# Delta attention: the first block products of an inverse on both halves of the partitions, and a new order on all five queues

## The chip, the cores and the metric

One core of one Trainium2 chip runs the whole program. The metric is the device time in microseconds (us) of one execution; the kernel before took 3255.22 us, the median of 3 executions (3253.78 to 3260.65).

## What is computed

The program is a small network on x of shape (4, 1024, 128), all in fp32. Its first and longest layer is a gated delta rule with 8 heads and 3 rank-one updates per token; a mixture of 15 experts, a decay attention and a second mixture follow and are not touched. Cut to what matters, per head and batch:

```python
for t in range(1024):
    S = S * exp(g[t])
    for i in range(3):                       # nh = 3 updates
        kS = k[t, i] @ S
        S = S + beta[t, i] * outer(k[t, i], v[t, i] - kS)
    o[t] = q[t] @ S
```

Before it come projections of x, a causal convolution of 4 taps on each of q, k and v, SiLU and a norm; behind it a norm, a gate and an output projection.

## The kernel before

The function `delta_attention` works in chunks of TC = 32 tokens. With 3 updates a token a chunk has R = 96 rows. A step N takes one head and NCC = 2 chunks of all B = 4 batches, so U = 8 units; there are NS = 128 steps (8 heads by 16). For each unit a 96 x 96 triangular matrix has to be inverted, after which the chunk is a few matrix products with the state S.

The inverse is made in blocks of BLK = 32. The three diagonal blocks are inverted on POOL (`subst`, lines 723 and 726) by forward substitution, for GROUP = 4 steps at a time: 31 pairs of a product and a subtraction, spread over four loop turns by `sub_steps` in 12 spots a turn. They go to DRAM and back (`n_d`, `x_d`, `y_d`), and on the way ACT transposes them once per group (`xt`, line 863). TensorE then joins the blocks: `zm` (line 1204) makes 64 x 64 products for each unit into the PSUM tile ZW, ACT moves them negated into Zt (`zev`, lines 844 and 845), `wm` (line 1213) multiplies Zt with Yf, ACT moves a part (`w12`, line 851), `m3` (line 1221) makes the last block, and `yev` (line 857) moves it to Yf. ZW has 128 x (8 x 64) fp32, one bank of PSUM, of which only partitions 0 to 63 are used.

The loop is a software pipeline. Turn f works on three steps at once: f (projections and taps of k and q), f - 1 (norms, Gram matrix, `kr`, `ap`, stores), c = f - BACK = f - 11 (v, gate, inverse blocks) and r = c - 1 (the recurrence on the state: `ks`, `rhs_`, `w_`, `wev`, `sr`, `sup`, `o_`), plus the output of r - 1. There are NF = 142 turns. In turns 0 to 10 only the k side is live, in turns 12 to 127 everything, from 128 on only the v side and the recurrence.

Each engine runs its queue strictly in the order in which the loop body lists the helpers, and waits at a helper's semaphores (`need`, `wait_ge`); the order is written out by hand for SP (all DMAs), POOL, ACT, DVE and PE. Things that the order has to respect:

- PP has two banks. Tiles v0, v2, k0, k2 use the first, v1, gate, k1, q (k_tile 3) the second; each projection overwrites what the tile before it in that bank left, so `k_tile(f, 1)` waits for ACT's `gate_(c)` (semaphore gate_ev) and `k_tile(f, 3)` for the third tap of k1.
- Each of the 7 convolved tiles needs tap 0 on ACT (line 788) and taps 1 to 3 on DVE (line 953), each tap waiting for the one before.
- TG holds transposes of k (`ktr`), of v (`vtr`) and the Gram matrices (`gram`), in two halves of four units.
- `xt` waits until the group's substitution is finished; the store of `y_d` on SP waits for `xt`.

The loads of the inverse blocks that the change touches (SP):

```python
sp.dma_start(apkB[N % 2][:, :, :], apk_d[slot(N)])...            # L601
for b in range(2):
    o = slice(BLK * b, BLK * (b + 1))
    sp.dma_start(Dd[N % 2][o, :, o], x_d[q, lanes(N, b)]...)...   # L605
```

## Time and profile before

| | |
|---|---|
| median of 3 executions | 3255.22 us |
| the profiled execution | 3252.41 us, its span 3250.6 us |
| busy over the span | PE 94%, DVE 78%, ACT 70%, POOL 60% |
| TensorE clock granted, mean | 0.963 |
| DMA engines busy, mean | about 56% |

The profile is of one execution. A "busy" PE is the union of its matmuls, whose ends are modelled; the start times are the reliable part, and the text mostly uses distances from start to start. PEld is the weight load that belongs to a matmul. An fp32 matmul is two instructions, so the eight products of `zm` are 16 rows. By the slices of the page the delta layer lies between about 100 and 2480 us, and from about 240 to 2350 us all slices look alike.

### The profile page before, as it was taken

The numbers are of one execution on the slowest core, as the hardware profiler recorded it, in microseconds if no ns is written. First come the engines' busy times: TensorE is split into PE (matmuls) and PEld (weight loads), VectorE is DVE, ScalarE is ACT, GpSimd is POOL, SyncE is SP. The second block draws the span as 40 slices with busy tenths as digits, with TensorE's granted clock in tenths as the row PEclk, the third lists the DMA queues.
The fourth block names the chain that finished last, engine by engine and source line by source line (L and its number), as shares of the span: only waits on it lengthen the run. The fifth ranks groups of instructions, "written<-read, shape, count | busy, mean of one in ns | idle before, by whom it ended". The sixth has DMA issues, their size and how long they took to land. (4 is left out here: it accounts for less than half of the span.)

```text
span 3250.6 us, 83664 instructions
## 1 busy us (share of the span) xinstructions
PE 3046.8 (94%) x27404; PEld 2373.9 (73%) x27404; DVE 2528.6 (78%) x5801; ACT 2265.4 (70%) x6879; POOL 1956.2 (60%) x3107
## 2 busy tenths in 40 slices
PE   5669999999999999999999999999998999768998
PEld 3458888888888888888888888888775444455444
DVE  5669999999999999999999999999654444684443
ACT  4678888888888888888888888888543333323333
POOL 1588888888888888888888888888720000100000
PEclk8779999999999999999999999999998999869999
DMA  4356776767677676767767677766532232002323
GB/s 100 113 153 172 186 183 174 181 173 182 168 190 179 176 181 169 182 174 188 182 170 183 171 175 178 190 180 165 141 95 83 107 145 98 10 2 76 147 98 124
DMA packets 587912, 482.88 MB, mean 149 GB/s; under 512 B 464492, under 2 KB 504076, under 8 KB 581340
## 3 DMA queue, kind: packets, MB, share of 16 engines
q1 hardware_dynamic: 587484, 477.53, 55.5%
q8 instruction: 225, 3.69, 0.5%
q14 instruction: 203, 1.66, 0.2%
HBM read 285.52 MB, written 191.86 MB: 147 GB/s over the span
## 5 line engine op out<-in xcount | busy, mean ns | idle before, releaser
L953 DVE SCALAR_TENSOR_TENSOR conv_k<-PP,tk,conv_k 128x256 f32<-128x256 f32 x1536 | 723.4, 479 | 62.9 <-ACT conv_k L788 35.1
L726 POOL TENSOR_TENSOR X<-X,tmp 96x31 f32<-96x31 f32 (+15 forms) x992 | 534.1, 538 | 77.7
L953 DVE SCALAR_TENSOR_TENSOR conv_v<-PP,tv,conv_v 128x256 f32<-128x256 f32 x1152 | 539.4, 477 | 45.1 <-ACT conv_v L788 35.5
L723 POOL TENSOR_TENSOR tmp<-At,X 96x31 f32<-96x31 f32 (+15 forms) x992 | 486.1, 490 | 63.0 <-DMA At<-n_d 4.8
L1122 PE MATMUL PP<-xn,wk 128*128 128x268 f32 x1024 | 344.6, 421 | 33.7 <-DVE conv_k L953 25.1
L709 POOL TENSOR_TENSOR rk<-ss,half 96x8 f32<-96x8 f32 x128 | 209.5, 1637 | 175.3 <-DVE ss L921 175.3
L691 POOL TENSOR_TENSOR Sg<-S,gend 128x512 f32<-128x512 f32 x256 | 266.1, 1039 | 59.3 <-DVE S L912 59.3
L760 ACT ACTIVATE recA<-TG,es 96x128 f32<-96x128 f32 x1024 | 284.9, 368 | 8.7 <-DVE es L946 8.7
L788 ACT ACTIVATE conv_k<-PP,tk 128x256 f32<-128x256 f32 x512 | 245.1, 480 | 60.1 <-PE PP L1122 53.4
L752 ACT ACTIVATE recA<-TG 128x128 f32<-128x128 f32 x1024 | 265.5, 272 | 25.3 <-PE TG L1173 25.3
L1086 PE MATMUL RB<-rhs,Yf 96*96 96x128 f32 x2048 | 269.1, 274 | 14.6 <-DVE rhs L901 14.3
L778 ACT ACTIVATE ws<-RB 96x512 f32<-96x512 f32 x256 | 151.6, 592 | 183.0 <-PE RB L1086 180.2
L1076 PE MATMUL RA<-S,kqgB 128*96 128x128 f32 x2048 | 276.2, 278 | 1.0 <-DVE S L912 1.0
L1096 PE MATMUL RA<-ws,recB 96*128 96x128 f32 x2048 | 271.1, 275 | 0.2 <-ACT ws L778 0.2
L1086 PEld LDWEIGHTS RB<-rhs,Yf 96*96 96x96 f32 x2048 | 242.2, 163 | 37.0 <-DVE rhs L901 24.6
L1096 PEld LDWEIGHTS RA<-ws,recB 96*128 96x128 f32 x2048 | 259.2, 192 | 8.0 <-ACT ws L778 0.8
L1185 PE MATMUL TG<-kq 128*96 128x128 f32 x1888 | 245.3, 273 | 1.2 <-ACT recA L760 1.0
L1076 PEld LDWEIGHTS RA<-S,kqgB 128*96 128x96 f32 x2048 | 233.4, 163 | 13.0 <-DVE S L912 4.4
L676 POOL TENSOR_TENSOR kqgA<-kq,gdec 128x768 f32<-128x768 f32 x128 | 203.2, 1588 | 39.3 <-ACT kq L829 32.6
L1122 PE MATMUL PP<-xn,wv 128*128 128x268 f32 x768 | 218.5, 391 | 2.3 <-DVE conv_k L953 2.3
L1185 PEld LDWEIGHTS TG<-kq 128*96 128x96 f32 x1888 | 219.0, 163 | 2.2 <-ACT recA L760 2.2
L1122 PEld LDWEIGHTS PP<-xn,wk 128*128 128x128 f32 x1024 | 163.8, 200 | 64.5 <-issue 34.5
(280 smaller groups left out, 6787.9 us busy)
## 6 DMA issues: line engine op xcount, KB each, us to landing
kqg_d<-kqgA SPq DMA_DIRECT2D x128, 512.0 KB, 6.2
kqgB<-kqg_d SPq DMA_DIRECT2D x128, 512.0 KB, 4.3
rec_d<-recA SPq DMA_DIRECT2D x128, 480.0 KB, 3.4
recB<-rec_d SPq DMA_DIRECT2D x128, 480.0 KB, 5.8
f1gates<-f1gates_d SPq DMA_DIRECT2D x24, 1024.0 KB, 6.7
f2gates<-f2gates_d SPq DMA_DIRECT2D x24, 1024.0 KB, 6.7
gdec<-gdec_d SPq DMA_DIRECT2D x128, 128.0 KB, 5.6
apk_d<-apkA SPq DMA_DIRECT2D x128, 128.0 KB, 3.3
```

The lines of the kernel that those rows point to most:

```text
L691: nc.gpsimd.tensor_tensor(Sg[:, :, :], S[cc][:, :, :], d.broadcast_to([128, B, 128]), ALU.mult).then_inc(sg_ev[cc], 1)
L723: nc.gpsimd.tensor_tensor(t, At[q % 2][:, j, j + 1:].unsqueeze(2).broadcast_to(sh), X[q % 2][:, j, 0:cols].unsqueeze(1).broadcast_to(sh), ...
L726: nc.gpsimd.tensor_tensor(x, x, t, ALU.subtract).then_inc(sub_ev, 1)
L752: last = nc.scalar.activation(recA[N % 2][:, u * 128:(u + 1) * 128], TG[:, u, :], ACT.Square, accum_out=ksum[:, u:u + 1])
L760: last = nc.scalar.activation(recA[N % 2][0:R, u * 128:(u + 1) * 128], TG[0:R, u, :], ACT.Copy, scale=es[:, u, TC - 1:TC])
L788: nc.scalar.activation(acc, src[:, :, 0:SPAN], ACT.Copy, scale=w).then_inc(tap0_ev[i], 1)
L953: return nc.vector.scalar_tensor_tensor(acc, src[:, :, j:j + SPAN], w[:, j:j + 1], acc, ALU.mult, ALU.add)
L1076: last = mm(RA[0:R, b, :], kqgB[N % 2][:, b * NCC + cc, 0:R], S[cc][:, b, :], start=True, stop=True)
L1086: last = mm(RB[0:R, b, :], Yf[N % 2][:, b * NCC + cc, :], rhs[:, b, :], start=True, stop=True)
L1096: last = mm(RA[:, b, :], recB[N % 2][:, u * 128:(u + 1) * 128], ws[cc][:, b, :], start=True, stop=True)
L1122: mm(out, w, x, start=True, stop=True).then_inc(tile_mm[i], 1)
L1185: last = mm(gram_bank(N, hf)[0:R, u % HU, :], kq[N % 2][:, u, 0:R], kq[N % 2][:, u, :], start=True, stop=True)
```

## The change

`zm` no longer puts all eight units on partitions 0 to 63. Units 0 to 3 stay there and units 4 to 7 go to partitions 64 to 127 of apkB, Dd and ZW, and the matmuls alternate between the halves, so that they address two row tiles (and with them two column tiles) of the array. The loads of apkB and Dd become 2 + 4 DMAs where there were 1 + 2, of half the size each. ACT's move into Zt becomes four instructions, two for each half. `wm` and `m3` stay as they are and still use partitions 0 to 63 of ZW.

All five loop bodies have a new order. On PE `o_(r, 1)` moves behind the next turn's first v tile, `vtr(c, 0)` too, and `m3` no longer follows `o_(r, 1)` but stands between `k_tile(f, 3)` and `w_(r, 1)`; the Gram products swap. On ACT `xt` moves from the head of the turn to just ahead of `gate_`. On POOL the last substitutions of a group run in the next turn. On DVE `vr(c, 0)` moves into the next turn and `ap` swaps its halves. SP loads first and stores last.

```diff
--- before.py
+++ after.py
@@ -429,7 +429,7 @@
 
         kqgB = two("kqgB", [128, U, 128])
         recB = two("recB", [R, U * 128 + U * TC])
-        apkB, Dd = two("apkB", [64, U, 64]), two("Dd", [64, U, 64])
+        apkB, Dd = two("apkB", [128, HU, 64]), two("Dd", [128, HU, 64])
         Yf = two("Yf", [R, U, R])
         Zt = sb("Zt", [R, U, 64])
         vt = sb("vt", [128, U, R])
@@ -598,11 +598,14 @@
                 need(sp, zm_mm, N - 2)
                 sp.wait_ge(preset_ev, 1)
                 sp.wait_ge(st_ap[N % 2], 4 * uses(N))
-                sp.dma_start(apkB[N % 2][:, :, :], apk_d[slot(N)]).then_inc(ld_da[N % 2], 16)
+                for hf in range(2):
+                    sp.dma_start(apkB[N % 2][64 * hf:64 * hf + 64, :, :], half(apk_d[slot(N)], hf)).then_inc(ld_da[N % 2], 16)
                 sp.wait_ge(st_x[q % 2], uses(q))
                 for b in range(2):
                     o = slice(BLK * b, BLK * (b + 1))
-                    sp.dma_start(Dd[N % 2][o, :, o], x_d[q, lanes(N, b)].rearrange("u r c -> r u c")).then_inc(ld_da[N % 2], 16)
+                    for hf in range(2):
+                        rows = slice(64 * hf + BLK * b, 64 * hf + BLK * b + BLK)
+                        sp.dma_start(Dd[N % 2][rows, :, o], x_d[q, lanes(N, b)][hf * HU:(hf + 1) * HU].rearrange("u r c -> r u c")).then_inc(ld_da[N % 2], 16)
 
             def y_load(N):
                 if not live(N):
@@ -639,16 +642,16 @@
 
             for f in range(NF):
                 r, c = f - BACK - 1, f - BACK
+                rec_load(c)
                 at_load(*group_at(f, GROUP + 1))
                 x_store(*group_at(f, 2 * GROUP + 1))
-                rec_load(c)
+                dec_load(f)
                 da_load(c + 1)
                 weights(*divmod(f, KSTEPS))
-                dec_load(f)
-                kqg_store(f - 1)
+                y_load(c + 1)
                 rec_store(f - 1)
                 ap_store(f - 1)
-                y_load(c + 1)
+                kqg_store(f - 1)
 
         @block.gpsimd
         def _(pool):
@@ -730,14 +733,15 @@
             nc.gpsimd.memset(S[0][:, :, :], 0.0).then_inc(preset_ev, 1)
             for f in range(NF):
                 r, c = f - BACK - 1, f - BACK
+                fo_(r - 1)
+                sg(r, 0)
+                subst(*group_at(f - 1, GROUP + 1), range(10, 12))
+                kqg(f - 1)
+                rk_(f - 1)
+                sg(r, 1)
+                subst(*group_at(f, GROUP + 1), range(0, 9))
                 x_zero(*group_at(f, 3))
-                fo_(r - 1)
-                kqg(f - 1)
-                sg(r, 0)
-                rk_(f - 1)
-                subst(*group_at(f, GROUP + 1), range(0, 6))
-                sg(r, 1)
-                subst(*group_at(f, GROUP + 1), range(6, 12))
+                subst(*group_at(f, GROUP + 1), range(9, 10))
 
         @block.scalar
         def _(act):
@@ -841,8 +845,10 @@
                 need(act, zm_mm, N)
                 need(act, m3_mm, N - 1)
                 act.wait_ge(preset_ev, 1)
-                nc.scalar.activation(Zt[32:64, :, 0:32], ZW[0:32, :, 0:32], ACT.Copy, scale=-1.0)
-                nc.scalar.activation(Zt[64:96, :, :], ZW[32:64, :, :], ACT.Copy, scale=-1.0).then_inc(zev_ev, 1)
+                for hf in range(2):
+                    nc.scalar.activation(half(Zt, hf)[32:64, :, 0:32], ZW[64 * hf:64 * hf + 32, 0:HU, 0:32], ACT.Copy, scale=-1.0)
+                    last = nc.scalar.activation(half(Zt, hf)[64:96, :, :], ZW[64 * hf + 32:64 * hf + 64, 0:HU, :], ACT.Copy, scale=-1.0)
+                last.then_inc(zev_ev, 1)
 
             def w12(N):
                 if not live(N):
@@ -864,27 +870,27 @@
 
             for f in range(NF):
                 r, c = f - BACK - 1, f - BACK
-                xt(*group_at(f, 2 * GROUP + 1))
                 tap0(c, "v0")
+                mo_(r - 1, 1)
+                ksum_(f - 1, 1)
                 tap0(c, "v1")
-                ksum_(f - 1, 1)
                 ksum_(f - 1, 0)
                 wev(r, 0)
                 tap0(c, "v2")
+                xt(*group_at(f, 2 * GROUP + 1))
                 gate_(c)
                 zev(c)
                 tap0(f, "k1")
                 mo_(r, 0)
                 tap0(f, "k0")
+                kr(f - 1, 1)
                 kr(f - 1, 0)
+                w12(c)
+                q2_(f - 1)
+                tap0(f, "k2")
+                tap0(f, "q")
                 vsilu(c)
-                kr(f - 1, 1)
-                tap0(f, "k2")
-                w12(c)
                 wev(r, 1)
-                q2_(f - 1)
-                tap0(f, "q")
-                mo_(r, 1)
                 yev(c)
                 ksilu(f)
                 qsilu(f)
@@ -1020,10 +1026,11 @@
             for f in range(NF):
                 r, c = f - BACK - 1, f - BACK
                 tap1(c, "v0")
+                tap2(c, "v0")
+                vr(c - 1, 0)
+                tap3(c, "v0")
                 osb_(r - 1)
-                tap2(c, "v0")
                 rhs_(r, 0)
-                tap3(c, "v0")
                 tap1(c, "v1")
                 og_(r - 1)
                 tap2(c, "v1")
@@ -1031,30 +1038,29 @@
                 ss_(f - 1)
                 rinv_(f - 1)
                 acc_(r - 1)
+                step_(f - 1)
                 tap1(c, "v2")
-                step_(f - 1)
                 tap2(c, "v2")
                 tap3(c, "v2")
+                es_(f - 1)
                 sup(r, 0)
-                es_(f - 1)
                 tap1(f, "k1")
+                tap2(f, "k1")
                 tap1(f, "k0")
                 tap2(f, "k0")
                 tap3(f, "k0")
+                tap3(f, "k1")
                 rhs_(r, 1)
-                tap2(f, "k1")
-                ap(f - 1, 0)
-                tap3(f, "k1")
+                ap(f - 1, 1)
                 tap1(f, "k2")
                 tap2(f, "k2")
-                ap(f - 1, 1)
                 tap3(f, "k2")
                 tap1(f, "q")
                 tap2(f, "q")
                 tap3(f, "q")
                 vr(c, 1)
+                ap(f - 1, 0)
                 sup(r, 1)
-                vr(c, 0)
 
         @block.tensor
         def _(pe):
@@ -1198,10 +1204,12 @@
             def zm(N):
                 if not live(N):
                     return
-                pe.wait_ge(ld_da[N % 2], 3 * uses(N))
+                pe.wait_ge(ld_da[N % 2], 6 * uses(N))
                 need(pe, yev_ev, N - 1)
-                for u in range(U):
-                    last = mm(ZW[0:64, u, :], apkB[N % 2][:, u, :], Dd[N % 2][:, u, :], start=True, stop=True)
+                for u in range(HU):
+                    for hf in range(2):
+                        o = slice(64 * hf, 64 * hf + 64)
+                        last = mm(ZW[o, u, :], apkB[N % 2][o, u, :], Dd[N % 2][o, u, :], start=True, stop=True)
                 last.then_inc(zm_mm, 1)
 
             def wm(N):
@@ -1238,8 +1246,10 @@
             for f in range(NF):
                 r, c = f - BACK - 1, f - BACK
                 v_tile(c, 0)
+                o_(r - 1, 1)
+                ktr(f - 1, 1)
+                vtr(c - 1, 0)
                 v_tile(c, 1)
-                ktr(f - 1, 1)
                 ks(r, 0)
                 ktr(f - 1, 0)
                 zm(c)
@@ -1254,15 +1264,13 @@
                 k_tile(f, 0)
                 wm(c)
                 ks(r, 1)
+                gram(f - 1, 1)
+                k_tile(f, 2)
+                k_tile(f, 3)
+                m3(c)
+                w_(r, 1)
                 gram(f - 1, 0)
-                k_tile(f, 2)
-                w_(r, 1)
-                gram(f - 1, 1)
-                k_tile(f, 3)
-                o_(r, 1)
-                m3(c)
                 vtr(c, 1)
-                vtr(c, 0)
                 sr(r, 1)
```

## Rows read from the trace of the kernel before

**Rows 1.** Windows view of 1000 to 1500 us: length, each engine's busy time.
```profile
core 0: us, PE busy (x) PEld busy (x) DVE busy (x) ACT busy (x) POOL busy (x), PEclk, DMA share, GB/s
1000.00:1500.00 500.00, 498.20 (x5078) 432.83 (x5081) 460.01 (x1075) 428.13 (x1386) 424.79 (x675) 1.00 0.72 179
```
**Rows 2.** Source view of `zm` (line 1204), 990 to 1500 us.
```profile
L1204 PE MATMUL ZW<-Dd,apkB x464: 218/218/267, 998.8 to 1495.6; 64*64 64x64 f32 x155
```
**Rows 3.** Waits view, 1000 to 1500 us: total us, times, longest.
```profile
PEld PP L1122 <- DVE conv_v L953: 3.4, 7, 0.5
PEld RB L1086 <- DVE rhs L901: 2.9, 7, 0.4
```
**Rows 4.** Timeline of PE in one steady turn: start, length of the group, instructions.
```profile
1016.28 1.14 PE L1204 MATMUL ZW<-Dd,apkB 64*64 64x64 f32 x16
1017.35 0.44 PE L1229 MATMUL SD<-ident,osb 128*128 128x128 f32 x2
...
1020.72 0.62 PE L1122 MATMUL PP<-xn,wk 128*128 128x268 f32 x2
1021.27 0.45 PE L1111 MATMUL SD<-S,kqgB 128*32 128x128 f32 x8
...
1021.87 0.72 PE L1122 MATMUL PP<-xn,wk 128*128 128x268 f32 x2
1022.52 1.15 PE L1213 MATMUL ZW<-Yf,Zt 96*64 96x64 f32 x16
...
1025.42 0.62 PE L1122 MATMUL PP<-xn,wk 128*128 128x268 f32 x2
1025.88 1.04 PE L1086 MATMUL RB<-rhs,Yf 96*96 96x128 f32 x8
...
1028.18 0.45 PE L1111 MATMUL SD<-S,kqgB 128*32 128x128 f32 x8
...
1028.64 0.67 PE L1221 MATMUL ZW<-Yf,Zt 96*32 96x32 f32 x16
1029.24 1.08 PE L1195 MATMUL TG<-ident,vt 128*96 128x128 f32 x8
...
1033.80 0.38 PE L1204 MATMUL ZW<-Dd,apkB 64*64 64x64 f32 x3
```
**Rows 5.** Timeline of PE in the decay attention: 64 x 64 products on four tiles.
```profile
2810.83 1.16 PE L1720 MATMUL b_pair<-b_rF,b_kB 64*64 64x64 f32 x64
2811.92 0.44 PE L1663 MATMUL b_pair<-ident,xT 128*128 128x128 f32 x2
```
**Rows 6.** Timeline of ACT in the same steady turn.
```profile
1019.20 0.46 ACT L788 ACTIVATE conv_v<-PP,tv 128x256 f32<-128x256 f32 x1
1020.02 0.38 ACT L810 ACTIVATE gate<-PP 128x256 f32<-128x256 f32 x1 [0.37 <-PE PP L1122]
1020.43 0.37 ACT L844 ACTIVATE Zt<-ZW 32x256 f32<-32x256 f32 x1
1020.82 0.59 ACT L845 ACTIVATE Zt<-ZW 32x512 f32<-32x512 f32 x1
...
1031.23 2.02 ACT L863 ACTIVATE At<-X 96x1024 f32<-96x1024 f32 x1
```
**Rows 7.** Timeline of SP's queue, same turn: the loads of Dd.
```profile
1018.44 1.08 SPq L605 DMA_DIRECT2D Dd<-x_d  x2
```
**Rows 8.** Timeline of one turn of the start-up.
```profile
156.20 0.42 DVE L946 TENSOR_TENSOR es<-edec,step_s 96x256 f32<-96x256 f32 x1
...
158.51 1.26 PE L1122 MATMUL PP<-xn,wk 128*128 128x268 f32 x2 [3.57 <-DVE conv_k L953]
...
161.27 1.10 PE L1122 MATMUL PP<-xn,wk 128*128 128x268 f32 x2
...
164.47 0.42 ACT L829 ACTIVATE kq<-conv_k 128x256 f32<-128x256 f32 x1 [0.41 <-DVE conv_k L953]
```
**Rows 9.** Timeline of PE in one turn of the run-out.
```profile
2415.16 1.14 PE L1204 MATMUL ZW<-Dd,apkB 64*64 64x64 f32 x16
...
2423.64 1.11 PE L1086 MATMUL RB<-rhs,Yf 96*96 96x128 f32 x8 [0.78 <-DVE rhs L901]
...
2425.43 0.45 PE L1111 MATMUL SD<-S,kqgB 128*32 128x128 f32 x8 [0.68 <-ACT ws L778]
...
2430.29 1.14 PE L1204 MATMUL ZW<-Dd,apkB 64*64 64x64 f32 x16
```

## The prediction

> **What bounds the kernel now.** I read the windows view first, for the long middle of the delta layer. PE is busy 498.20 of 500 us at full clock, DVE 460, ACT 428, POOL 425 [rows 1]. So PE has no gap to speak of, and the others have 1.4 to 2.6 us of slack in a turn. Next the source view of `zm`, which gives the beat: 464 rows are 29 turns of 16, the first starts at 998.8 and the last row of the last turn at 1495.6, about 0.98 behind its first; (1494.6 - 998.8) / 28 = 17.71 us a turn [rows 2]. The timeline of one turn then gives 1033.80 - 1016.28 = 17.52 us [rows 4]. Three turns in four take that, and the fourth, the one in which ACT runs `xt`, takes 4 x 17.71 - 3 x 17.52 = 18.28. The waits view shows that PE's own waits are short: 3.4 and 2.9 us in 28 turns, seven times each, one turn in four [rows 3]. Conclusion: the kernel is set by the length of PE's instruction stream, plus 0.76 us in every fourth turn in which `xt` (2.02 us [rows 6]) holds up ACT's taps. There are 116 full turns (f = 12 to 127, by the code), 10 turns of start-up and 11 of run-out, which have other bounds.
>
> **Part 1, zm on two row tiles.** `zm` starts at 1016.28 and the next group at 1017.35: 1.07 us for 16 instructions [rows 4]. The direct evidence for what tiles do is in the decay attention: 64 instructions of the very same shape, on four tiles, take 2811.92 - 2810.83 = 1.09 us [rows 5]. So four tiles run side by side, each at the pace of the single tile, and neither the weight loads nor the issue are in the way at 17 ns an instruction. Of the 1.07 us some 0.14 is the way out (next part), so a round takes (1.07 - 0.14) / 16 = 0.058 us; two tiles need 8 rounds less, **-0.47 us** a turn. Bounds: 0 (the tiles do not overlap) and -0.47. I take -0.47, as rows 5 are the same shape.
>
> **Part 2, crossings between array shapes.** The timeline shows what a change of the stationary width costs. A k tile followed by `w_` takes 0.46 (1025.42 to 1025.88); followed by the 32-column `o_` it takes 0.55: **0.09 in**. `o_` followed by `m3`, also 32 columns, takes 1028.64 - 1028.18 = 0.46; followed by a k tile 1021.87 - 1021.27 = 0.60: **0.14 out**. That k tile then takes 0.65 up to `wm`, 0.10 more than the 0.46 and 0.09 in explain, which is a tail of the way out [rows 4]. Before, `o_(r, 1)` and `m3` share one stay in the narrow shape. After, `o_(r, 1)` leaves to `ktr` and `m3` enters alone behind a k tile and leaves to `w_`. That is one exit and one entry more: 0.14 + 0.09, and 0 to 0.20 of tails; **+0.34 us** taken, bounds 0.23 and 0.43. The other narrow groups keep their neighbours' shapes. PE's stream becomes 17.52 - 0.47 + 0.34 = 17.39 us.
>
> **Part 3, the other queues, in the three turns without xt.** ACT: from 0.37 us at 256 columns and 0.59 at 512 [rows 6] a half-sized pair takes about 0.27 + 0.37, so four take 1.28 where two took 0.96: +0.32 on an engine with 2.5 us of slack. `wm` waits for it. With w_(r, 0) at 4.8 us into the turn, ws, tap v2 and gate end at about 7.6, the four moves at about 8.95, and `wm` starts at 9.7: covered, by 0.7. DVE: same instructions. `vr(c-1, 0)` fits while DVE waits for `ks` and `ot`, and I find the third tap of each tile ready before the PE tile that wants its bank, the tightest being v1 ahead of the gate tile, at the same distance as before. POOL: same work, its tail moved by some 1.2 us into the next turn. SP: three more DMA issues of about 0.54 us each (1.08 for two [rows 7]), +1.6 us on a queue that otherwise waits; the loads are for the next turn and land with 2 us or more in hand. Cost 0 for all four; if one of these covers is gone, the smallest margin (0 to 0.1 us at the gate tile) is what turns into waits.
>
> **Part 4, xt.** It moves ahead of `gate_`. In the old turn tap v2 starts at 1019.20 and the gate at 1020.02 [rows 6]. With `xt` between them the gate starts at 1019.20 + 0.40 + 1.92 = 1021.52, 1.50 later. PE's k1 tile, which overwrites the gate's bank, starts at 1020.72, 0.24 behind the earliest time that the gate's end (1020.40) allows. So PE stands 1.26 us in every fourth turn, where `xt` cost 0.76 before: **+0.50 in four turns, +0.125 a turn**. Bounds +0.40 and +0.65. Sum of a full turn: -0.47 + 0.34 + 0.125 = **-0.005 us**, over 116 turns -1 us; by the bounds of parts 2 and 4 from -16 to +13.
>
> **Part 5, start-up.** Here a turn is a loop of latencies: es, taps, SiLU, transposes, sums, es. From es (156.20) to the SiLU of q (164.47) are 8.27 us, and the q tile comes 2.76 behind the k2 tile because a Gram product stands between them [rows 8]. After, q follows k2 directly. The k2 tile is itself 0.5 late, as k0's taps come behind two taps of k1. Then DVE's six taps run without a pause, and I count 7.6 to the SiLU of q: -0.65 us for 10 turns, **-6.5** (0 to -13).
>
> **Part 6, run-out.** A turn takes 2430.29 - 2415.16 = 15.13 us, in which PE waits 0.78 for rhs and 0.68 for ws [rows 9]. After, `m3` fills 0.6 of the first wait, the second shrinks by about 0.2, `zm` gives 0.47, the crossings take 0.34, and the longer move into Zt some 0.2: -0.75 for 10 turns, **-7.5** (+2 to -12).
>
> **Sum.** -1 - 6.5 - 7.5 = -15 us on the profiled execution of 3252.4, 3237.4; the median lies 2.8 above that execution. I say 3238.
>
> **The rivals.**
>
> (A) Forecast: the turn is level, the ends gain. 3238, its own range 3216 to 3248. For it: the matching tile rows [rows 5] and a PE without gaps [rows 1].
>
> (B) Level in all: the crossings cost their upper end (+0.09 x 116 = +10) and the start-up gives nothing (+6.5): about 3254, inside 0.2%. For it: every term is of the size of the error of reading starts.
>
> (C) Slower, as the two row tiles do not overlap. The four tiles of rows 5 write their row halves to different banks of PSUM (the h index of the tile), whereas here both halves write one bank, ZW. If TensorE holds one row tile until the other's writes are out, the 0.47 is lost in all 138 live turns: 3238 + 54 for the full turns + about 4 at the run-out, **3296**. It decides if `zm` to `ot` stays above 0.9 us. Against it: in `o_`, four column tiles of one bank run side by side (16 instructions of 128 columns in 0.60 us [rows 4]). The Trainium skill ("TensorEngine Tiling (Array Packing)", section "Restrictions and Gotchas") says that different row tiles cannot access the same PSUM bank at the same time and leaves it to software. By it this layout is unsafe or serial; no row before the change shows two row tiles in one bank, so its chance is small but not nil.
>
> (D) Slower by new waits. DVE is at 92% [rows 1], and a hole of 0.2 us in each turn, at the gate tile or at k0 behind v2's taps, would lengthen every full turn: 3238 + 23 and no gain at the ends, about 3272. It decides from 0.12 us a turn on.
>
> **How the numbers follow.** A 0.62, B 0.19, C 0.06, D 0.13. A measurement tells apart about 0.2%, 6.5 us. Faster (below 3248.7): A without its rim, 0.62. Same: 0.19 and a rim of D, 0.20. Slower: 0.18. The range runs from 3212 (A with the lower ends of parts 2, 4, 5 and 6) to 3265, which takes in B and part of D and leaves out C.
>
> **What would show it.** In the profile after: `zm` to the next group 0.6 us with 16 rows (C: above 0.9); `o_(r, 1)` to `ktr` about 0.60, k3 to `m3` 0.55; three turns at 17.4 and one at 18.65, a mean of 17.7; in the waits view a line of PE waiting for ACT's gate, about 1.2 us once in four turns. If that line is missing, part 4 is wrong and the kernel is some 15 us faster than I say. If the turns without `xt` are above 17.5, look for PE waiting for DVE. Start-up turns should shrink by 0.5 to 1 us, run-out turns from 15.13 to about 14.4.

## The result, and the profile after

The changed kernel takes 3358.03 us (median of 4 executions, 3356.31 to 3361.34) against 3257.93 for the kernel before in the same runs: a ratio of 1.031, 95% interval 1.0292 to 1.0327. It is 100 us slower. I had forecast 3238, with a range up to 3265. The profiled execution took 3356.31 us, its span 3354.5.

The window that was read before, read again:

```profile
core 0: us, PE busy (x) PEld busy (x) DVE busy (x) ACT busy (x) POOL busy (x), PEclk, DMA share, GB/s
1000.00:1500.00 500.00, 476.79 (x4859) 401.45 (x4859) 457.31 (x1027) 412.75 (x1384) 405.66 (x647) 1.00 0.64 171
```

PE was busy 498.20 us there [rows 1] and is busy 476.79 now, at the same granted clock, with 4859 instructions in the window in place of 5078. Every engine has fewer instructions in it: the turns have become longer and PE stands. The source view of `zm` (line 1212 now; durations are those of single instructions in ns):

```profile
L1212 PE MATMUL ZW<-Dd,apkB x432: 218/218/268, 1002.6 to 1485.6; 64*64 64x64 f32 x144
```

These are 27 turns of 16 rows where there were 29 [rows 2]. From the start of one `zm` to the next, over turns 12 to 127, by the place of the turn in its group of four (the third column is the turn in which `xt` costs time; the kernel before runs it at the end of the turn ahead, 14.9 us behind that turn's `zm`):

| | plain | plain | turn of xt | turn behind it | mean |
|---|---|---|---|---|---|
| before | 17.52 | 17.52 | 18.28 | 17.52 | 17.71 |
| predicted | 17.39 | 17.39 | 18.65 | 17.39 | 17.71 |
| after | 17.86 | 17.74 | 18.65 | **20.13** | 18.60 |

0.89 us in 116 turns are 103 us, the whole loss. The waits view of 1000 to 1500 us (total us, times, longest) has lines that are new or much longer, chosen here from the view; before, PE waited 3.4 us for conv_v and 2.9 for rhs [rows 3], and DVE's osb 2.2 us for fo:

```profile
engine line waited for: us in total, times, longest us
POOL tmp L726 <- DMA At<-n_d: 18.8, 7, 3.4
PEld PP L1128 <- DVE conv_v L959: 13.4, 18, 1.1
DVE osb L1006 <- POOL fo L705: 9.8, 7, 2.1
PEld PP L1128 <- ACT gate L814: 8.2, 7, 1.2
PEld SD L1237 <- DVE osb L1006: 5.8, 7, 1.6
```

Seven times in 27 turns is once in a group of four. Three things stand here. The gate line is `xt`, forecast as about 1.2 us once in four turns. The conv_v line is in the turns without `xt`. The lines for At, fo and osb are one chain: POOL waits for the DMA that brings At, so its `fo` comes late, so DVE's osb, so PE's transpose of osb.

The timeline of PE (start, length, instructions, wait before it) shows that the array did what I had worked out:

```profile
1037.32 0.45 PE L1117 MATMUL SD<-S,kqgB 128*32 128x128 f32 x8
...
1037.92 0.66 PE L1179 MATMUL TG<-ident,kq 128*128 128x128 f32 x4
...
1040.71 0.68 PE L1212 MATMUL ZW<-Dd,apkB 64*64 64x64 f32 x16
1041.32 0.44 PE L1237 MATMUL SD<-ident,osb 128*128 128x128 f32 x2
```

`zm` to the next group is 0.61 us with all 16 rows (it was 1.07 [rows 4]; 0.60 was forecast). `o_(r, 1)` to `ktr` is 1037.92 - 1037.32 = 0.60, as forecast. So the loss does not lie in how long `zm` and the crossings take.

### The profile page after: what moved, and what is told of

Read it like the earlier page. It is cut to its first block and busy times, and to the rows that moved or that the text cites. A ratio compares the mean times of both kernels' runs of the same rounds, so it can differ in the third digit from the quotient of the medians.

```text
span 3354.5 us, 84304 instructions
## 1 busy us (share of the span) xinstructions
PE 3044.4 (91%) x27404; PEld 2316.8 (69%) x27404; DVE 2607.7 (78%) x5801; ACT 2279.5 (68%) x7135; POOL 1954.1 (58%) x3107
## 5 line engine op out<-in xcount | busy, mean ns | idle before, releaser
L959 DVE SCALAR_TENSOR_TENSOR conv_k<-PP,tk,conv_k 128x256 f32<-128x256 f32 x1536 | 707.1, 481 | 117.1 <-ACT conv_k L792 84.5
L959 DVE SCALAR_TENSOR_TENSOR conv_v<-PP,tv,conv_v 128x256 f32<-128x256 f32 x1152 | 549.7, 477 | 22.2 <-ACT conv_v L792 3.9
L1128 PE MATMUL PP<-xn,wk 128*128 128x268 f32 x1024 | 324.1, 421 | 118.4 <-DVE conv_k L959 43.6
L1092 PE MATMUL RB<-rhs,Yf 96*96 96x128 f32 x2048 | 282.0, 281 | 7.4 <-DVE rhs L907 5.6
L1128 PEld LDWEIGHTS PP<-xn,wk 128*128 128x128 f32 x1024 | 171.2, 196 | 170.0 <-DVE conv_v L959 56.2
L792 ACT ACTIVATE conv_k<-PP,tk 128x256 f32<-128x256 f32 x512 | 230.0, 474 | 83.1 <-PE PP L1128 76.1
L764 ACT ACTIVATE recA<-TG,es 96x128 f32<-96x128 f32 x1024 | 274.0, 371 | 7.7 <-DVE es L952 7.7
L1082 PEld LDWEIGHTS RA<-S,kqgB 128*96 128x96 f32 x2048 | 240.8, 163 | 22.9 <-DVE S L918 0.9
L1092 PEld LDWEIGHTS RB<-rhs,Yf 96*96 96x96 f32 x2048 | 235.3, 164 | 23.2 <-DVE rhs L907 18.2
L1128 PE MATMUL PP<-xn,wv 128*128 128x268 f32 x768 | 241.5, 395 | 0.0
L756 ACT ACTIVATION_READ_ACCUMULATOR recA<-TG 128x1 f32 x1024 | 213.4, 208 | 0.0
```

Of the source, the lines that this page charges most:

```text
L756: last = nc.scalar.activation(recA[N % 2][:, u * 128:(u + 1) * 128], TG[:, u, :], ACT.Square, accum_out=ksum[:, u:u + 1])
L764: last = nc.scalar.activation(recA[N % 2][0:R, u * 128:(u + 1) * 128], TG[0:R, u, :], ACT.Copy, scale=es[:, u, TC - 1:TC])
L792: nc.scalar.activation(acc, src[:, :, 0:SPAN], ACT.Copy, scale=w).then_inc(tap0_ev[i], 1)
L959: return nc.vector.scalar_tensor_tensor(acc, src[:, :, j:j + SPAN], w[:, j:j + 1], acc, ALU.mult, ALU.add)
L1082: last = mm(RA[0:R, b, :], kqgB[N % 2][:, b * NCC + cc, 0:R], S[cc][:, b, :], start=True, stop=True)
L1092: last = mm(RB[0:R, b, :], Yf[N % 2][:, b * NCC + cc, :], rhs[:, b, :], start=True, stop=True)
```

## The experiments

Each time is a median; the ratio is to the kernel before in the same runs, with its 95% interval. The turns are in the order of the table above: plain, plain, turn of `xt`, turn behind it.

| run | us | ratio | turns | mean |
|---|---|---|---|---|
| e1_tiles_alone | 3239.84 | 0.9958 (0.9939 to 0.9978) | 17.10 17.09 18.28 17.56 | 17.51 |
| e2_orders_alone | 3360.57 | 1.0317 (1.0302 to 1.0332) | 17.87 17.86 19.11 19.74 | 18.64 |
| e3_at_first | 3284.97 | 1.009 (1.007 to 1.011) | 17.86 17.73 18.66 17.69 | 17.98 |
| e4_kqg_later | 3594.75 | 1.1028 (1.0971 to 1.1085) | 20.32 20.47 19.54 20.86 | 20.30 |
| e5_kqg_behind_sg | 3312.92 | 1.0182 (1.0158 to 1.0207) | 17.40 17.40 18.65 19.34 | 18.20 |
| e6_xt_at_head | 3318.2 | 1.019 (1.0167 to 1.0213) | 17.4 17.4 18.68 19.64 | 18.28 |
| e7_tiles_xt_halves | 3221.46 | 0.9896 (0.9864 to 0.9928) | 17.11 17.09 17.09 18.04 | 17.33 |
| e8_xt_halves_alone | 3244.89 | 0.9963 (0.9949 to 0.9977) | 17.52 17.52 17.52 17.77 | 17.58 |
| e9_at_late_before | 3362.75 | 1.0317 (1.0299 to 1.0335) | 17.52 17.52 18.28 21.04 | 18.59 |
| e10_kqg_ahead | 3276.76 | 1.0063 (1.0047 to 1.0079) | 17.41 17.41 19.47 17.40 | 17.92 |
| e11_kqg_ahead_halves | 3244.84 | 0.9961 (0.9947 to 0.9976) | 17.42 17.40 18.47 17.41 | 17.67 |
| e12_tail_behind_sg | **3192.82** | **0.9803** (0.9787 to 0.9819) | 17.10 17.09 17.33 17.13 | 17.16 |

Where `xt` is cut in two, the third number is the turn of its first half and the fourth that of its second.

**The two halves of the change.** e1_tiles_alone is the changed kernel with the loop bodies of the kernel before on all five queues: only the row tiles, their loads and the four moves into Zt are left. e2_orders_alone is the kernel before with the new loop bodies.

> The kernel before with the row-tile form of zm (its split loads and four moves into Zt) and nothing else; all five loop bodies are in their old order. Theory (tiles help, the new orders cost): zm to its successor falls from 1.07 to 0.61 us, the three plain turns from 17.52 to about 17.06, the fourth by about as much; 0.46 x 126 turns = 58 us off, about 3198 us, ratio 0.982. Rival 1 (the tile form itself carries the loss, through 3 more DMA issues and 2 more ACT instructions a turn): plain turns stay at 17.5 or rise, ratio 1.00 to 1.03. Rival 2 (DVE or ACT becomes the bound as soon as PE's stream is shorter): part of the gain, plain turns at 17.3, ratio about 0.99.

> The kernel before with the five new loop bodies and the old zm on partitions 0 to 63. Theory (the orders carry the whole loss and zm lies on the chain ot, og, taps, so its 0.47 us counts in every turn): turns about 0.45 us longer than in the changed kernel, mean about 19.0, about 3410 us, ratio 1.047. Rival (PE waits anyway in these turns, so a longer zm is swallowed by the waits): mean turn stays at 18.6, about 3360 us, ratio 1.03. Rival 2 (tiles are at fault): near the kernel before, ratio 1.00.

The tiles alone give 0.43 us in the two plain turns (17.52 to 17.09) and a kernel that is 16 us faster, where 58 were expected. In the turn of `xt` (18.28) and behind it (17.56) the gain does not show: the waits view of e1 has PE waiting 5.5 us for rhs in 7 waits, one turn in four, where it was 2.9. That leaves 0.20 x 116 = 23 us. The start-up gives 6 more (first `zm` at 216.4, before at 222.2). The run-out takes 13 back, and that is mostly TensorE's clock. In the windows view the third figure from the end of a line is the granted clock: 1.00 is the upper of its two levels, 2.4 GHz, and a mean below 1.00 says that part of the stretch ran at the lower one, 1.2 GHz. A run-out turn of the kernel before, then one of e1, then one of e7, which has the same tiles:

```profile
2400.00:2415.20 15.20, 13.67 (x150) 11.61 (x149) 8.86 (x19) 6.65 (x15) 3.03 (x5) 1.00 0.34 92
2380.11:2397.15 17.04, 14.96 (x149) 12.57 (x148) 8.79 (x19) 6.98 (x17) 2.97 (x5) 0.90 0.32 82
2304.10:2319.60 15.50, 13.42 (x149) 11.12 (x148) 8.81 (x19) 7.37 (x18) 10.44 (x23) 1.00 0.42 109
```

In each of e1's last eight run-out turns the clock falls behind PE's waits of 0.78 us for rhs and 0.68 for ws, and the turn takes 17.04 us; with the clock granted in full it is 15.5.

The new orders alone cost as much as the whole change. Their first plain turn takes 17.87 us where the changed kernel's takes 17.86, although `zm` takes 1.07 us there and 0.61 here. The windows view of one such turn of e2 shows why:

```profile
1045.67:1063.52 17.85, 17.85 (x181) 15.25 (x180) 16.49 (x39) 14.62 (x49) 15.57 (x23) 1.00 0.61 157
```

In e2 PE does not wait in this turn: its stream in the new order is 17.87 long, 0.35 more than before, which is the crossings measured by themselves. With the tiles the stream is 0.47 shorter, and PE stands for what they gave. In the turn of `xt` the tiles do show (19.11 against 18.65), and the turn behind it takes that back (19.74 against 20.13).

**At's load.** The turn behind `xt` is the dearest. The source view of At's load, before and after (the last line is the time from the issue to the landing):

```profile
L624 SPq DMA_DIRECT2D At<-n_d x7: 381/382/503, 1033.7 to 1458.8; - x7
DMA to landing us min/median/max: 3.6/3.8/4.2
```
```profile
L627 SPq DMA_DIRECT2D At<-n_d x7: 330/406/418, 1005.1 to 1449.6; - x7
DMA to landing us min/median/max: 6.7/6.8/7.4
```

The timeline of SP and POOL in the changed kernel shows why:

```profile
1003.24 0.45 SPq L564 DMA_DIRECT2D kqg_d<-kqgA  x1
1003.79 0.37 SPq L590 DMA_DIRECT2D kqgB<-kqg_d  x1
1004.21 0.79 SPq L592 DMA_DIRECT2D recB<-rec_d  x1
1005.10 0.42 SPq L627 DMA_DIRECT2D At<-n_d  x1
...
1011.91 0.23 POOL L726 TENSOR_TENSOR tmp<-At,X 96x31 f32<-96x31 f32 x1 [2.44 <-DMA At<-n_d]
```

The load is issued 1.9 us behind `kqg_store` (512 KB by the page of the profile) and directly behind the two loads of `rec_load`, which bring 512 and 480 KB. By the page's medians these two take 4.9 and 6.3 us to land, which puts them at about 1008.7 and 1010.5; At lands behind them, at about 1011.9. It takes 3.0 us longer to land than it did, counted from its own issue. POOL needs it at 1009.5 and gets it at 1011.9. e3_at_first moves two lines of SP and nothing else, the load of At and the store of kqg; no run moves only one of them, so their shares are not told apart:

```diff
-                rec_load(c)
                 at_load(*group_at(f, GROUP + 1))
+                rec_load(c)
...
+                kqg_store(f - 1)
                 y_load(c + 1)
                 rec_store(f - 1)
                 ap_store(f - 1)
-                kqg_store(f - 1)
```

> The changed kernel with two moves on SP: the load of At stands ahead of rec_load's two loads, and the store of kqg ahead of y_load. Theory (At lands late because three large transfers of 512, 512 and 480 KB stand ahead of it; POOL idles some 2.4 us in the xt turn and carries that into the next turn, where fo, osb and then PE's ot come late): POOL's wait for At falls from 18.8 us in 500 us to under 5, the turn behind the xt turn falls from 20.1 to about 18.0, the others stay; 2.1 x 29 = 61 us off, about 3297 us, ratio 1.012. Rival (POOL is late in that turn because of its own work, memset and large substitutions): less than 15 us off.

3284.97 us: 73 us of the 100 are gone, the landing is back at 3.7 us (median), and the turn behind `xt` falls from 20.13 to 17.69. The other three turns do not move. e9_at_late_before is the reverse, the kernel before with SP's loop in the order of the changed one (`dec_load` alone keeps its old place):

> The kernel before, with nothing changed but the order of SP's loop, which is that of the changed kernel. If the late load of At is enough by itself to cost time, the group's first substitution waits on POOL here too, POOL carries some 2.4 us over the end of that turn, and the turn behind it is about 2 us longer: mean turn about 18.2 us, 3310 us in all. The rival says that it needs POOL's new order as well, in which less of POOL's idle time lies ahead of the next turn's fo: then POOL catches up inside the same turn, the turns stay 17.52, 17.52, 17.52 and 18.28, and the time is 3255 to 3265.

3362.75 us. The order of one queue of DMA issues, with all else as before, costs 105 us, and its turns are those of the kernel before but for the one behind `xt`, which goes from 17.52 to 21.04. So the rival, that POOL's new order is needed as well, is refuted. The waits view of e9, 1000 to 1500 us, has the same chain:

```profile
DVE osb L1000 <- POOL fo L702: 18.1, 7, 3.2
POOL tmp L723 <- DMA At<-n_d: 15.9, 7, 2.9
PEld SD L1229 <- DVE osb L1000: 8.3, 7, 1.8
```

The turn costs 3.52 us more than before, where late At costs 20.13 - 17.69 = 2.44 in the changed kernel, though POOL waits a little less for At (15.9 us against 18.8). The difference goes with the clock. Two turns behind `xt` of e9, by the windows view:

```profile
1018.27:1037.69 19.42, 18.10 (x181) 15.33 (x181) 17.32 (x41) 14.87 (x49) 18.09 (x26) 1.00 0.65 159
1091.00:1112.45 21.45, 19.49 (x181) 16.69 (x181) 17.22 (x41) 14.97 (x49) 19.91 (x29) 0.92 0.54 132
```

The same 181 rows keep PE busy 1.4 us longer in the second. Its timeline of PE shows the waits, and behind them a group that takes 1.06 us where it takes 0.59 in the first turn:

```profile
1093.55 0.44 PE L1229 MATMUL SD<-ident,osb 128*128 128x128 f32 x2 [1.42 <-DVE osb L1000]
1094.53 1.20 PE L1086 MATMUL RB<-rhs,Yf 96*96 96x128 f32 x8 [0.54 <-DVE rhs L901]
...
1096.43 1.06 PE L1236 MATMUL SD<-og,wo 128*128 128x256 f32 x2
```

Taken over the 28 turns behind `xt` that the table averages, e9 has 10 with the clock granted in full, 19.62 us in the mean, and 18 with less, 21.83. In the changed kernel these are 23 turns of 19.93 and 5 of 21.05; the kernel before and e3 have none with less. At full clock, then, a late At costs about the same in both: 19.62 - 17.52 = 2.10 and 19.93 - 17.69 = 2.24. Of e9's 105 us at least 18 x 1.4 = 25 are PE's slower matmuls, an estimate from the two turns above.

**The plain turns.** After e3 they are still 17.86, 17.73 and 17.69, where the stream of PE without waits would be about 17.4. The timeline of DVE and POOL in one turn of the changed kernel:

```profile
1041.91 1.58 POOL L679 TENSOR_TENSOR kqgA<-kq,gdec 128x768 f32<-128x768 f32 x1
...
1043.11 1.09 DVE L927 TENSOR_SCALAR ss<-ksum 128x8 f32<-128x8 f32 x1
...
1043.46 0.71 POOL L680 TENSOR_TENSOR kqgA<-kq,gdec 128x256 f32<-128x256 f32 x1
```

`ss` works on 8 columns and takes 1.09 us. It starts during POOL's first product of kqg and does not end with it (1041.91 + 1.58 = 1043.49) but at 1044.20, when the second one ends (1044.17). By the lines view of DVE, split by shape, 1000 to 1500 us (count, then busy us and mean ns), first before and then after:

```profile
L921 DVE TENSOR_SCALAR ss<-ksum 128x8 f32<-128x8 f32 x29 | 4.7, 162 | 0.0
```
```profile
L927 DVE TENSOR_SCALAR ss<-ksum 128x8 f32<-128x8 f32 x27 | 28.3, 1050 | 0.0
```

From 162 to 1050 ns in the mean, and in no turn below 297 (by the view of the tile ss, 297 to 1826). In the kernel before, `kqg` stood ahead of `sg(r, 0)` and was done when `ss` came; now it stands behind `sg(r, 0)` and two spots of substitution and meets it. DVE's taps of v2 follow `ss`, and PE's k0 tile waits for them (the conv_v line above). Three runs move POOL's `kqg`: e4 in the changed kernel, e5 and e10 on top of e3 (e5 moves two spots of substitution with it).

e4_kqg_later has it one helper later, behind `rk_`:

```diff
-                kqg(f - 1)
                 rk_(f - 1)
+                kqg(f - 1)
                 sg(r, 1)
```

> The changed kernel with kqg and rk_ swapped on POOL, so that POOL waits for ss instead of running the 128 x 768 product while DVE issues ss. Theory (DVE's ss, 1050 ns here and 162 ns before, is held until POOL's product is done, which delays v2's taps and with them PE's k0 tile): ss back to about 0.16 us, PE's waits for conv_v at the k tile gone, the two turns of 17.86 and 17.74 fall to about 17.4; about 25 to 35 us off, about 3328 us, ratio 1.021. Rival (ss is long for another reason, such as waiting for ksum): ss stays near 1 us and the time stays within 5 us.

It is 237 us slower than the changed kernel. `ss` is short again there, 0.16 us in all 25 turns of the window, and the lines view shows what is held in its place:

```profile
L943 DVE TENSOR_TENSOR step_s<-rinv,beta 96x8 f32<-96x8 f32 x25 | 53.1, 2124 | 0.0
```

`step_` is a product of 8 columns from two SBUF inputs, 0.15 us when nothing of this kind runs on POOL; here it lasts until `rk_` is over (1.2 us) or, in most turns, the products of `kqg` behind it as well (2.6 us). Not all of the 237 us is this. Three plain turns of e4 by the windows view, with `step_` at 1.2, 2.65 and 2.65 us:

```profile
1130.09:1148.24 18.15, 17.46 (x181) 14.78 (x180) 17.13 (x39) 14.79 (x51) 15.80 (x23) 1.00 0.58 151
1148.24:1167.85 19.61, 17.47 (x182) 14.79 (x181) 18.65 (x39) 14.79 (x51) 14.51 (x25) 1.00 0.65 159
1389.19:1410.36 21.17, 19.03 (x182) 16.31 (x181) 18.99 (x39) 15.05 (x51) 14.47 (x25) 0.92 0.49 134
```

The longer `step_` costs 1.46 us, and the fall of the clock behind PE's wait 1.56 more. In 33 of the 57 plain turns both are there, 21.1 to 22.8 us long. e5_kqg_behind_sg is e3 with `kqg` behind `sg(r, 1)`, clear of both:

```diff
-                kqg(f - 1)
                 rk_(f - 1)
+                subst(*group_at(f, GROUP + 1), range(0, 2))
                 sg(r, 1)
-                subst(*group_at(f, GROUP + 1), range(0, 9))
+                kqg(f - 1)
+                subst(*group_at(f, GROUP + 1), range(2, 9))
```

> e3_at_first with one more change on POOL: kqg stands behind sg(r, 1) instead of ahead of rk_, and two of the substitution spots ahead of it, so that no 128 x 768 product of POOL runs while DVE has ss, step or es. Theory (a DVE instruction whose inputs are all in SBUF is held until POOL's large product ends): ss 0.16 us instead of 0.93, step 0.15 us, no PE wait for conv_v at the k tile, the two plain turns at 17.4 instead of 17.86 and 17.73; 0.4 x 87 turns, about 30 us less than e3, 3255 us, ratio 1.000. Rival (POOL is late again because 14.9 us of work now come in a worse order, and fo and osb are late in every turn): above e3's 3285 us.

The plain turns are 17.40 and 17.40, and `ss` is back:

```profile
L928 DVE TENSOR_SCALAR ss<-ksum 128x8 f32<-128x8 f32 x28 | 4.5, 161 | 0.0
```

The time is nevertheless 28 us longer than e3's and 58 above the 3255 expected: one turn in four went from 17.69 to 19.34. POOL now needs At earlier, before `sg(r, 1)`, waits for it and is late for `fo`. Its waits view:

```profile
POOL tmp L726 <- DMA At<-n_d: 10.9, 7, 2.4
...
DVE osb L1007 <- POOL fo L705: 6.4, 7, 1.7
```

Of the 28 turns behind `xt` 19 have the clock in full and take 18.42 us; 9 have not and take 21.31. At full clock the longer turn (+0.73) and the two shorter ones (-0.46 and -0.33) about cancel, and 9 x 2.89 = 26 us, nearly the whole distance to e3, lie in the nine turns.

e10_kqg_ahead puts `kqg` where the kernel before had it, ahead of `sg(r, 0)`, on top of e3:

```diff
                 fo_(r - 1)
+                kqg(f - 1)
                 sg(r, 0)
                 subst(*group_at(f - 1, GROUP + 1), range(10, 12))
-                kqg(f - 1)
                 rk_(f - 1)
```

> e3_at_first (changed kernel with At's load issued first) with POOL's kqg moved ahead of sg(r, 0), directly behind fo, where the kernel before had it. The theory that the plain turns of the changed kernel are 0.3 to 0.46 us longer than its TensorE stream only because POOL's large product runs beside DVE's ss says: ss is back at about 0.16 us, the plain turns are 17.40, the turn of xt stays 18.65, and the mean is 17.7 to 17.8: 3250 to 3262 us. The rival says that the plain turns are set by the new places of the taps on DVE and stay at 17.74 to 17.86: 3280 to 3290 us.

All three turns without `xt` are 17.40, as the theory says, though `ss` is at 0.39 us (median) and not at 0.16: two spots of substitution run beside it. The time is 3276.76, outside the 3250 to 3262 that I had given. The turn of `xt` went up, from 18.66 to 19.47. Its timeline of ACT shows the reason:

```profile
1047.60 1.99 ACT L869 ACTIVATE At<-X 96x1024 f32<-96x1024 f32 x1 [0.62 <-POOL X L729]
1049.47 0.38 ACT L814 ACTIVATE gate<-PP 128x256 f32<-128x256 f32 x1
```

The group's last two spots of substitution now stand behind `kqg`, `xt` waits 0.62 us for them, and PE waits for the gate 1.71 us in that turn. So none of the four places tried in these orders is free: ahead of `ss` `kqg` delays `xt`, beside `ss` or `step_` it holds DVE, behind them it delays the substitution and `fo`.

**The place and the size of xt.** e6_xt_at_head is e5 with `xt` at the head of the next turn and the store of y_d a turn later.

> e5_kqg_behind_sg with xt moved to the head of ACT's next turn, and the store of y_d with it. Theory (part 4 of the prediction: xt in front of the gate costs PE 1.25 us in one turn of four, at the head 0.76): no wait of PE for ACT's gate, xt's turn at about 18.2 instead of 18.65; 0.45 x 29 = 13 us less than e5, about 3242 us, ratio 0.996. Rival (at the head it delays mo, fo and osb instead, since these are tight in the new order): no better than e5, or slower.

It is no faster than e5 (3318.2 against 3312.92). PE's wait for the gate is gone, as expected, but the turn of `xt` takes 18.68 where 18.2 was expected: the 2 us of ACT cost about 1.25 us in a turn at either place, now as a wait of PE for vrow, 7.5 us in 7 waits. e7_tiles_xt_halves and e8_xt_halves_alone cut it instead, the one on top of e1, the other on the kernel before. Here is the edit on ACT (the comments are added here):

```diff
-                xt(*group_at(f, 2 * GROUP + 1))
...
+                xt(*group_at(f, 2 * GROUP + 1), 0)      # columns 0 to 15, 96 x 512
+                xt(*group_at(f, 2 * GROUP + 2), 1)      # columns 16 to 31, a turn later
                 wev(r, 0)
```

> e1_tiles_alone with xt cut into two halves of 96 x 512 that run in two successive turns in front of wev(r, 0), where ACT waits 0.8 us or more for PE; the store of y_d comes one turn later. Theory (what e1 loses is xt's 2 us at the head, 1.2 us in its turn and 0.5 in the next): all turns at 17.1 to 17.2, 1.5 x 29 = 43 us less than e1, about 3196 us, ratio 0.982. Rival (DVE, at 92% before, is the bound of turns that are this short): all turns at 17.3 to 17.5, ratio 0.99.

> The kernel before with the two halves of xt as in e7 and no row tiles. Theory: PE's stream of 17.52 us is the whole turn in all four, 0.76 x 29 = 22 us less than before, about 3234 us, ratio 0.993. If the halves do not fit into ACT's wait, the turns that hold them stay above 17.8 and the ratio is 0.997 or more.

The halves are worth 10 us on the kernel before (22 were expected), whose median in those runs was 3254.8 us, and take e1's 3239.84 to 3221.46 (3196 expected). What is left in e7 is one turn in four of 17.6 to 19.1, in which DVE waits for POOL's `fo` (4.5 us in 7 waits, longest 1.5); that is the turn at whose end POOL has the group's longest substitutions and clears X as well. e11_kqg_ahead_halves puts halves into e10, the first at `xt`'s place there:

> e10_kqg_ahead with xt cut in two halves of 96 x 512: the first where the changed kernel has xt, behind v2's tap and ahead of the gate, the second one turn later ahead of wev(r, 0); the store of y_d is one turn later. If the cost of xt is its length ahead of the gate, the turn of the first half is about 18.0 instead of 18.65 and the next one 17.4 to 17.6: mean 17.55 to 17.6, 3232 to 3240 us. The rival says that POOL's substitution, of which two steps lie in that turn, and not xt's length, releases ACT there: then the turn stays near 18.5 and the time within 10 us of e10.

3244.84 us: the turn of `xt` falls from 19.47 to 18.47. It missed the 18.0 that I had given, since the wait for POOL's X is still there (0.6 us) and half of `xt` still stands ahead of the gate; both of the expectation's mechanisms are at work. e12_tail_behind_sg goes after e7's last wait:

```diff
-                x_zero(*group_at(f, 3))
                 fo_(r - 1)
                 kqg(f - 1)
                 sg(r, 0)
+                subst(*group_at(f - 1, GROUP + 1), range(11, 12))
                 rk_(f - 1)
                 subst(*group_at(f, GROUP + 1), range(0, 6))
                 sg(r, 1)
-                subst(*group_at(f, GROUP + 1), range(6, 12))
+                subst(*group_at(f, GROUP + 1), range(6, 11))
+                x_zero(*group_at(f, 3))
```

On SP `rec_load` also moves ahead of `x_store`, while At's load stays first.

> e7_tiles_xt_halves (row tiles in the order of before, xt in halves) with the last spot of POOL's substitution and the clearing of X moved out of the way of the next turn's fo: the spot lies behind sg(r, 0), where POOL waited 1.4 us for ss, and x_zero at the end of the loop; SP loads the recurrence's tiles before it waits for the group's substitution. If POOL's overrun at the end of a group's turn is what makes one turn in four 17.6 to 19.1, that turn falls to 17.1 to 17.6 and the time to 3200 to 3210 us. The rival says that the store of x_d, now some 3 us later, and so the loads of Dd, or the first half of xt at the gate, take its place: 3220 us or more.

3192.82 us, 2.0% below the kernel before and better than I had given. Its window:

```profile
1000.00:1500.00 500.00, 500.00 (x5262) 432.36 (x5261) 475.32 (x1108) 452.25 (x1503) 439.17 (x705) 1.00 0.67 185
```

PE is busy 500.00 of 500 us, with 5262 instructions where the kernel before had 5078 [rows 1]. The moved spot fills part of the time in which POOL waited for `ss` (1.10 us are left of it), and in the waits view no line of osb waiting for `fo` is left:

```profile
1008.75 1.64 POOL L717 TENSOR_TENSOR rk<-ss,half 96x8 f32<-96x8 f32 x1 [1.10 <-DVE ss L936]
```

## Why the prediction was wrong, point by point

The loss of a group of four turns is 74.38 - 70.84 = 3.54 us. The runs divide it, in the order in which they take one part after another away; the terms were not measured each by itself:

| term | us in four turns | over 29 groups | from |
|---|---|---|---|
| PE's stream, 17.52 to 17.40 | -0.48 | -14 | e5, e10 |
| `xt` ahead of the gate, 1.25 in place of 0.76 | +0.49 | +14 | after, e3 |
| `ss` held by `kqg`, 0.46 + 0.34 + 0.29 | +1.09 | +32 | e3 against e5 and e10 |
| At's load late, 20.13 - 17.69 | +2.44 | +71 | e3, e9 |
| sum | +3.54 | +103 | |

**What bounds the kernel:** right, PE's stream; what the other queues had in hand was smaller than their busy shares suggest.

**Part 1** was right: -0.46 measured, -0.47 forecast. Rival C (3296) is refuted; the two row tiles overlap although both write ZW, one bank (1.07 us to 0.61). By the rule of the Trainium skill that I had weighed there ("TensorEngine Tiling (Array Packing)", "Restrictions and Gotchas") they should not share a bank at all; the 0.61 us shows no cost of it.

**Part 2** was right: a stream of 17.39 was forecast and 17.40 is what PE takes in e5 and e10 when nothing waits, and e2 gives the crossings alone as 17.87 - 17.52 = 0.35, forecast 0.34.

**Part 4** was right: 18.65 us for the turn of `xt` was forecast and 18.65 measured, with PE waiting 8.2 us in 7 turns, 1.2 each, for the gate.

**Part 3 is the step that failed**, in two of its four zeros. For SP I counted the three added issues at 0.54 us and wrote that the loads "land with 2 us or more in hand". I had looked at the loads that the change splits, not at the one it moves: At's load went from the head of the queue to behind a store and two loads. It was issued later and took 3.0 us longer to land, and POOL stood for it by 2.44 us in the turn shown, 2.7 in the mean (18.8 us in 7 waits). For POOL I wrote "same work", and for DVE "same instructions". Both are true and neither is a cost: where a POOL product falls in the DVE's order changes how long the DVE instruction takes. The trace of before held the evidence, in its start-up, where `kqg` does meet these instructions (timeline of DVE and POOL, kernel before):

```profile
153.73 2.44 DVE L937 TENSOR_TENSOR step_s<-rinv,beta 96x8 f32<-96x8 f32 x1
...
168.32 1.09 DVE L921 TENSOR_SCALAR ss<-ksum 128x8 f32<-128x8 f32 x1 [3.88 <-ACT recA L752]
```
```profile
153.90 1.57 POOL L676 TENSOR_TENSOR kqgA<-kq,gdec 128x768 f32<-128x768 f32 x1
...
167.80 1.58 POOL L676 TENSOR_TENSOR kqgA<-kq,gdec 128x768 f32<-128x768 f32 x1
```

2.44 and 1.09 us for operations of 0.15 and 0.16. I had read this stretch for Part 5 and not asked why they were long. The Trainium skill has the rule ("SBUF — State Buffer", "Who interferes with whom"): DVE and GpSimd share a pair of ports, a DVE instruction with two SBUF inputs contends with a GpSimd instruction that reads SBUF, a `tensor_scalar` can as well, and the later one is blocked for the whole of the other. The trace agrees that `step_` and `ss` are held. In places they are held for more than one instruction of POOL: `ss` at 1043.11 and `step_` at 153.73 outlast the first product of `kqg` and end with the second (1044.17 and 156.15), while `ss` at 168.32 ends with the first. That they wait for this port and for nothing else is the page's account; the runs show that the length follows the place of `kqg`.

Rival D had the right kind of loss and the right place ("at k0 behind v2's taps"), at 0.2 us a turn where 1.09 / 4 = 0.27 came, and it gave 3272 (its own terms, 3238 + 23 and no gain of 14 at the ends, come to 3275). The larger term, At, was in no rival.

**Part 5** was right in its turns and wrong in its sum. From es to es, eight start-up turns take 188.64 - 93.64 = 95.0 us where they took 102.6: -0.95 a turn, more than the -0.65 forecast. But the first `zm` starts at 221.8, against 222.2 before. All of it is lost in one turn, the one with the first `xt` (timeline of ACT, after):

```profile
195.29 1.96 ACT L869 ACTIVATE At<-X 96x1024 f32<-96x1024 f32 x1 [7.45 <-POOL X L729]
```

Start-up turns are 12 us long, POOL's substitution of a group is as long as ever, and ACT, with the taps of k queued behind `xt`, stands 7.45 us for it. That turn takes 23.2 us instead of 14.2. Part 4 priced `xt`'s place by its length alone, which holds only while the substitution is done in time; the same wait came back in e10 and e11.

**Part 6:** undisturbed run-out turns take 14.15 us (14.4 forecast), but three take 16.2, 20.3 and 19.0, so nothing is gained. Two of the three come of SP's order and of what the clock made of PE's waits, since e3, which differs in SP's order alone, has them shorter. The 20.3 turn, and the same turn in e3:

```profile
2425.60:2445.90 20.30, 16.19 (x149) 13.47 (x148) 9.18 (x19) 7.13 (x17) 13.40 (x23) 0.83 0.25 64
2357.40:2372.50 15.10, 13.41 (x149) 11.06 (x148) 9.03 (x19) 7.01 (x17) 10.71 (x19) 1.00 0.35 90
```

PE waits 3.71 us for osb in the first. The 19.0 turn has a clock of 0.82 and takes 16.5 at full clock in e3. The 16.2 turn is the same in e3, and its cause is open. The forecast had no term for the clock in the delta layer, where the kernel before shows 1.00 in every full turn.

**The sum.** Two slips do not bear on the outcome. The sum gives 3237.4 for the profiled execution, and with the 2.8 by which the median lay above it the forecast had to be 3240, not 3238. The bounds of parts 2 and 4 give -16 to +14, not +13.

Had Part 3's two zeros held, the turns would have been 17.40 three times and 18.65 once, 17.71 in the mean, exactly level with the kernel before. So even without its faults, this change as a whole would give back through `xt` and the crossings what its tiles gain; e1 keeps 0.43 us of it in plain turns, as it has no extra crossings.

## What to carry to other kernels

When a change redraws a DMA queue, list for each load what stood ahead of it before and what stands ahead of it now, and find who waits for it: one small load behind two large ones and a store cost more here than everything else together, while the engine counts were unchanged. When it redraws a POOL or DVE queue, lay the two timelines over each other and look for POOL's long SBUF products beside DVE's small operations; the shape of a DVE instruction does not give its time. When a wait of PE grows, read the granted clock of the turns behind it before the loss is put down to the wait. And take a change of several parts one at a time: the tiles were worth 16 us alone, and 64 us together with a halved `xt` and a moved POOL tail, and the new orders hid that completely.

## What was unexpected of the hardware

An 8-column `tensor_scalar` on DVE took 162 ns alone and 1050 in the mean beside the products of `kqg` on POOL, and an 8-column product took 150 ns or, in the mean of e4, 2124. The reciprocal between them took 0.20 us in every case seen, and DVE's 256-column taps, which read PSUM for one input, kept their 0.47. Beside POOL's shorter substitution products `ss` took 0.39 us (median) in e10. A load of the same size from the same place took 3.8 us to land at the head of SP's burst and 6.8 to 7.1 when issued directly behind about 1 MB of other loads, with a store of 512 KB ahead of them. And the granted clock fell behind waits of PE in many turns, not in all: in e9 behind 1.42 and 0.54 us, where it cost PE another 1.4 us, and in the run-out of e1 behind 0.78 and 0.68 us, in each of eight turns.
